# Routed experts of a mixture layer: weight rows dealt to SBUF partitions by neighbours instead of in blocks of 128

## The reference

```python
logits = x @ router_w.T                       # 800 tokens, 8 experts
top_vals, top_idx = jax.lax.top_k(logits, 1)  # one expert for each token
scores = sigmoid(top value for the chosen expert, 0 for the others)
xr = x[None] * scores.T[:, :, None]
gate_up = jnp.einsum('eth,ehf->etf', xr, gate_up_proj)      # 256 -> 2 x 512
gate, up = jnp.split(gate_up, 2, axis=-1)
routed = jnp.einsum('etf,efh->eth', up * silu(gate), down_proj)   # 512 -> 256
shared = silu(x @ shared_gate_w) * (x @ shared_up_w) @ shared_down_w
out = shared + routed.sum(axis=0)
```

## Time and profile before

| what | us |
|---|---|
| median of three runs | 1210.91 |
| the profiled execution, as timed | 1210.05 |
| its span in the profile | 1208.0 |
| PE busy | 1050.0 |
| first gate/up product of tile 0 | at 269.00 |
| first gate/up product of tile 13 | at 355.19 |
| median time from issue to landing, `egu` / `edn` | 5.6 / 6.4 |

### The profile page before, as it was taken

The page is one execution under the profiler, slowest core; times in us unless marked ns, Lnnn a source line. Parts: engine busy times, 40 slices in busy tenths (PEclk is TensorE's granted clock), DMA queues, the critical chain, the costliest instruction groups (busy, mean ns, idle before and its releaser), DMA issues.

```text
span 1208.0 us, 18195 instructions
## 1 busy us (share of the span) xinstructions
PE 1050.0 (87%) x6674; PEld 841.2 (70%) x6674; DVE 530.6 (44%) x1063; ACT 565.0 (47%) x1205; POOL 579.8 (48%) x787
## 2 busy tenths in 40 slices
PE   6986776788882879999999999999999999999883
PEld 3665665457872748888788678778778778877572
DVE  3234552333202663544743653563473473472423
ACT  2322222101212215765765664764665675577761
POOL 2002230244004007767676676676677575376760
PEclk9767887889996969999999999999999999999986
DMA  9015001516761000000000000000000000000000
GB/s 242 4 48 162 1 1 50 197 39 220 269 222 46 1 13 1 1 14 1 1 17 1 1 17 2 1 17 1 1 1 17 1 1 5 1 1 5 1 4 3
DMA packets 37827, 49.25 MB, mean 41 GB/s; under 512 B 9798, under 2 KB 31352, under 8 KB 37484
## 3 DMA queue, kind: packets, MB, share of 16 engines
q1 hardware_dynamic: 36716, 46.46, 12.4%
q0 software_dynamic: 1024, 1.64, 0.4%
HBM read 42.73 MB, written 5.31 MB: 40 GB/s over the span
## 4 chain that ended last, share of the span: by engine, by line
PE 61%; DVE 14%; issue 9%; POOL 6%; ACT 6%; DMA 2%; SPq 0%; POOLq 0%; DVEq 0%; ACTq 0%
PE ps L1033 8%; PE ps L990 5%; PE ps L972 5%; DVE nm L1654 5%; PE ps L913 4%; PE ps L1017 4%; PE ps L1047 4%; PE ps L1044 4%; PE ps L1045 4%; POOL pl L619 3%; PE ps L976 3%; PE ps L1075 2%; PE ps L1066 2%; PE ps L926 2%; PE ps L734 2%
## 5 line engine op out<-in xcount | busy, mean ns | idle before, releaser
L619 POOL TENSOR_TENSOR pl<-pt,ph 120x400 fp32r<-120x400 f32 (+1 forms) x384 | 407.5, 1081 | 282.4 <-ACT ph L1422 238.6
L1421 ACT ACTIVATE pt<-ps 120x400 f32<-120x400 f32 (+1 forms) x384 | 193.8, 505 | 154.3 <-PE ps L1033 150.7
L1654 DVE TENSOR_REDUCE nm<-ps 128x1 f32<-128x482 f32 (+1 forms) x312 | 184.1, 650 | 39.7 <-PE ps L1017 39.1
L1422 ACT ACTIVATE ph<-ps 120x400 fp32r<-120x400 f32 (+1 forms) x384 | 192.0, 500 | 0.0
L1033 PE MATMUL ps<-qh,khl 128*120 128x400 f32 (+1 forms) x384 | 149.7, 390 | 8.8 <-ACT ph L1422 5.6
L1033 PE MATMUL ps<-ql,kh 65*120 65x400 f32 (+1 forms) x384 | 135.1, 352 | 0.0
L1047 PE MATMUL ps<-pl,kv 120*65 120x400 f32 (+1 forms) x384 | 134.2, 349 | 0.4 <-POOL pl L619 0.2
L1044 PE MATMUL ps<-ph,kv 120*65 120x400 f32 (+1 forms) x384 | 134.2, 350 | 0.0
L1045 PE MATMUL ps<-ph,kv 120*64 120x400 f32 (+1 forms) x384 | 133.5, 348 | 0.0
L1017 PE MATMUL ps<-khl,qh 128*128 128x482 f32 (+1 forms) x312 | 101.5, 419 | 6.1 <-DVE ql L1646 1.7
L1633 DVE TENSOR_TENSOR xyz<-ps,ropeq 128x400 f32<-128x400 f32 x64 | 33.8, 570 | 157.3 <-PE ps L976 157.3
(11 more groups left out here) (250 smaller groups left out, 1592.8 us busy)
## 6 DMA issues: line engine op xcount, KB each, us to landing
egu<-_L_ffn_gate_up_proj_dram SPq DMA_DIRECT2D x14, 1024.0 KB, 5.6
edn<-in_L_ffn_down_proj_dram SPq DMA_DIRECT2D x14, 512.0 KB, 6.4
craw<-in_ctx_dram SPq DMA_DIRECT2D x8, 360.0 KB
wo_n<-in_L_xattn_Wo_dram SPq DMA_DIRECT2D x1, 2048.0 KB, 11.7
wq_n<-in_L_xattn_Wq_dram SPq DMA_DIRECT2D x1, 2048.0 KB, 9.7
xs_scratch<-zero SPq DMA_DIRECT2D x1, 1792.0 KB, 12.9
xs<-xs_scratch SPq DMA_DIRECT2D x14, 128.0 KB, 5.5
ys_scratch<-ysb SPq DMA_DIRECT2D x14, 128.0 KB, 5.8
```

Source lines behind the costliest of these rows:

```text
L619: nc.gpsimd.tensor_tensor(pl[k % PS_BUF][r, :], pt[k % PT_BUF][r, :], ph[k % PS_BUF][r, :].bitcast(F32), ALU.subtract).then_inc(pl_ready, 1)
L1421: nc.scalar.activation(pt[k % PT_BUF][0:rows, :], ps[0:rows, k % 2, 0:HT], ACT.Exp)
L1422: nc.scalar.activation(ph[k % PS_BUF][0:rows, :], ps[0:rows, k % 2, 0:HT], ACT.Exp).then_inc(ph_ready, 1)
L1654: nc.vector.tensor_reduce(nm3[0:w, i, n:n + 1], ps[0:w, max_bank(b, i) + n, 0:MN], AX.X, ALU.max)\
```

## The change

Three access patterns of the routed experts change together.

```diff
--- before.py
+++ after.py
@@ -390,8 +390,8 @@
             if t >= EBUF:
                 sp.wait_ge(t_down, t - EBUF + 1)
             e = sp.value_load(owner[0:1, t:t + 1], min_val=0, max_val=NE - 1)
-            sp.dma_start(egu[t % EBUF][:, :, :], gate_up[bass.ds(e, 1)].rearrange("a (c p) n -> p (a c) n", p=128)).then_inc(ld_e[t % EBUF], 16)
-            sp.dma_start(edn[t % EBUF][:, :, :], down[bass.ds(e, 1)].rearrange("a (m p) n -> p (a m) n", p=128)).then_inc(ld_e[t % EBUF], 16)
+            sp.dma_start(egu[t % EBUF][:, :, :], gate_up[bass.ds(e, 1)].rearrange("a (p c) n -> p (a c) n", p=128)).then_inc(ld_e[t % EBUF], 16)
+            sp.dma_start(edn[t % EBUF][:, :, :], down[bass.ds(e, 1)].rearrange("a (p m) n -> p (a m) n", p=128)).then_inc(ld_e[t % EBUF], 16)
 
         def load_slots(sp, t):
 
@@ -896,7 +896,7 @@
                 else:
                     pe.wait_ge(x_shared, B)
                 for c in range(DC):
-                    last = turn(ps[:, 4 + t % 2, TR * c:TR * c + TR], xs[t % XBUF][:, 128 * c:128 * c + 128], ident[:, :])
+                    last = turn(ps[:, 4 + t % 2, TR * c:TR * c + TR], xs[t % XBUF][:, c:D:DC], ident[:, :])
                 last.then_inc(xs_turned, 1)
 
             def expert_in(t, a):
@@ -911,7 +911,7 @@
                 for m in range(FM):
                     for c in range(DC):
                         last = mm(ps[:, 2 * (t % 2) + a, TR * m:TR * m + TR],
-                                  egu[t % EBUF][:, c, FI * a + 128 * m:FI * a + 128 * m + 128], xsT[t % 2][:, c, :],
+                                  egu[t % EBUF][:, c, FI * a + m:FI * a + FI:FM], xsT[t % 2][:, c, :],
                                   start=c == 0, stop=c == DC - 1)
                 last.then_inc(t_up if a else t_gate, 1)
```

## The result

Four runs of the changed kernel took 1247.72, 1244.75, 1248.07 and 1247.99 us, median 1247.86, against a median of 1210.93 for the kernel before (1206.18 to 1216.58, 4 runs). The ratio is 1.0297 with a 95% interval of 1.025 to 1.0344: slower by 37 us. The profiled execution took 1247.72 us. The forecast of 1209.1 and its range of 1200 to 1245 are both missed; rival 1 had 1242.6 (its sum as written, 1210.9 + 45 - 13.4, gives 1242.5).

A forecast was written before the change was run, and what follows sets the result against it. PE bounds the kernel (87% busy), with routed-expert periods set by weight loads. Loads 0.33 us shorter (0.15 + 0.18), half for 11 periods, give 1.8 us: 1210.91 - 1.8 = 1209.1 us against the median, range 1200 to 1245.

The forecast's parts named there:

- rival 1: PE, line 913: stepped load becomes the bound, pairs 220 ns instead of 119, total 1242.6 us; chance 0.26.
- I take 0: Line 913's gate/up operand with 16-byte step: no added cost assumed; bounds nothing to 144 us.
- time for two such reads: PE weight loads: bf16 element every 0.48 ns, fp32 every 0.86, so two reads were said to fit per fp32 element.
- slow clock of tile 3: Line 913 after tile 3's wait: 32 pairs took 5.44 us instead of 3.81; up to 1.63 sparable, taken 0.
- Down weights, 0.15 us a load: Down-weight loads, 1 KB to 4 KB pieces: 1.39 us becomes 1.24, 0.15 off each; bounds 0.12 and 0.25.
- gate/up start, 0.18: Gate/up weight loads, 8 KB pieces: slow start shortened by 0.18 us a load; bounds 0 and 0.77.
- The 1.8 us: Routed experts: total forecast gain, half of 0.33 us a load for 11 periods.
- the half of a load's gain for each period: Routed experts' two-tile loop: half of what a load gets shorter comes off each period, tiles 3 to 13.
- The loop of L and 5.75: Routed experts: period is (L + 5.75) / 2 or 5.59 us, whichever is more; L: down product's end to reloaded tile's start.
- rival 2: Line 913's waits vanish, periods go from 6.70 towards 5.59 us, up to 11.8 + 1.6 off, about 1201; chance 0.14.
- Turns with a step of 8 bytes, 0: Token turns, 28 single loads of 142 ns: no added cost taken; bound 0 to 4 us.
- GpSimd's all-reduce, 0: First all-reduce, starting at 240.80 after 7.92 us of issue: up to 1.6 us gain or as much cost, taken 0.

The follow-up runs named there:

- step of 2: Kernel before the change with only the gate/up operand reading every second column (8 bytes): 1213.05 us, ratio 1.0027.
- step 3: Kernel before the change with only the gate/up operand reading every third column (12 bytes): 1226.51 us, one run.
- experiment 4: Kernel before the change plus 4 KB down-weight pieces and gate/up operand step of 16 bytes; gate/up weights and tokens as before: 1247.19 us, ratio 1.0309.
- experiment 2: Kernel before the change plus larger pieces for both weights and tokens turned with a step; gate/up operand read without step: 1212.14 us, ratio 0.9996.
- experiment 12: Against a kernel issuing gate/up weights a tile earlier (1208.06 us), token loads also issued earlier, ahead of the weights: 1197.97 us, ratio 0.9878.
- experiment 1: Kernel before the change with only the gate/up operand read with a step of 16 bytes: 1246.1 us, ratio 1.030.

## Why the prediction was wrong

**The step that failed is "I take 0" for the gate/up operand with a step of 16 bytes.** It was argued from the bf16 loads' 62 ns for 128 columns, as if the reader could fetch a new address every 0.48 ns. Those columns lie beside each other, 8 to a line of 16 bytes: 16 lines in 62 ns, 3.9 ns for each line. The loads that the prediction set out reach one line in 3.4 ns at best (32 lines in the 110 of the earlier trace rows); the change asks for 128. The row was near by the count of elements, but lines were what had to be counted. Even by elements it fell short of "time for two such reads": 0.86 / 0.48 is 1.8. In place of 0 the step measured 51.0 us of PE time (105.7 - 54.7 for line 913), 236 ns a pair over all 448 (105.7 / 448), 2.0 times the 119 ns pair and 2.1 times the 110 ns load; rival 1 had the factor 2.

The Trainium skill (Advanced Engine Details and Errata, "SBUF Cachelines"), which the prediction set against its own value, was right in kind: different line, penalty. Its sentence that two hits on a line absorb the latency agrees with the step of 2 (126 ns) and with step 3, where two of three lines are hit once only and the price is 63 ns a pair. The runs give it the size that it lacks: 1.8 to 1.9 ns a line.

**Rival 1, point by point.** It had pairs of 220 ns, and 242 were measured in tile 0 (236 over all); 3.2 us more a tile, and 3.90 were measured (7.74 - 3.84); the issue waits of 11.8 us and the slow clock of tile 3 given back, which both happened. With tile 0's time its sum is 14 x 3.90 - 13.4 = 41.2 us, against 38.0 of the stretch; with the busy time of the whole line, in which the slow clock of before is already counted, it is 105.7 - 54.7 - 11.8 = 39.2. It also named the threshold, 30 ns a pair: step 2 (6 ns) stays inside it and costs 0.27%, step 3 (63 ns) is outside and costs 16 us in one run. Its chance of 0.26 was too low, and the range, cut at 1245 against a dearer load, was short by 3.

**Down weights, 0.15 us a load; gate/up start, 0.18.** With loads well apart, by the count over all reloads in experiment 4, 4 KB down weights are worth 0.14 to 0.29 us, and the 8 KB pieces 0.02 more (0.08 by the medians), together 0.16 to 0.31 where 0.33 was forecast. So the term for the down weights is borne out, and the term for the start, a middle between two guesses, is not: hardly anything is left for it. In the kernel's own rhythm (experiment 2) no gain is seen: the same count has a mean of 7.23 us, with two loads of over 9, where it was 6.83 before, and the total is the same to within 4 us. Loads there are issued before the one ahead has landed, as the timeline of experiment 2 shows:

```profile
314.10 0.34 SPq L393 DMA_DIRECT2D egu<-_L_ffn_gate_up_proj_dram  x1
...
314.95 3.81 PE L913 MATMUL ps<-xsT,egu 128*128 128x128 f32 x32 [1.58 <-issue]
...
321.44 0.34 SPq L393 DMA_DIRECT2D egu<-_L_ffn_gate_up_proj_dram  x1
...
321.99 1.24 PE L913 MATMUL ps<-xsT,egu 128*128 128x128 f32 x9 [1.27 <-issue]
```

Tile 7 starts at 314.95, 0.85 us after the weights of tile 8 were asked for, and tile 8 then 7.89 us after the asking. That this overlap eats the gain is likely and was not isolated. The 1.8 us, and with them the half of a load's gain for each period, stay neither shown nor refuted.

**The loop of L and 5.75.** Right as to what the waits are: taking the load out of the loop takes the period to 5.52 (5.59 forecast as PE's own pace) and 13.5 us off the total (11.8 + 1.6 = 13.4 was rival 2's bound). What the prediction did not see is the second wait behind the first: the tokens, asked for after the weights on one queue, which held nearly all of it until experiment 12.

**Turns with a step of 8 bytes, 0.** Right for the time, although the loads themselves got longer (median 209 ns in the changed kernel, 144 in experiment 1): periods with them and without are 9.31 each in the changed kernel and in experiment 1 ((388.35 - 285.90) / 11 and (387.91 - 285.53) / 11). **GpSimd's all-reduce, 0:** it started at 239.70 after 8.35 us of issue in the changed kernel, against 240.80 after 7.92; nothing to tell from noise.

## What to carry to other kernels

Before an operand of PE is given a step, count the 16-byte lines under it, not its elements, and hold lines x 1.8 to 1.9 ns against the time its product has anyway: 64 lines hid under 120 ns, 96 didn't. Longer pieces of a DMA gave 0.2 to 0.3 us a load here and nothing that the total shows, while an earlier issue of the same loads and of the tokens gave 13.5 us; look first at what releases the buffer, and at what is asked for behind the load on the same queue.

## What the runs showed of the hardware that was not expected

The price of a line does not follow PE's clock. Line 913 alone (window; length, busy and count of PE, of PEld; granted clock, DMA share, GB/s), first in the changed kernel, then in the kernel before. The counts take in the products that a window's edges cut:

```profile
269.80:271.80 2.00, 2.00 (x10) 2.00 (x10) 0.50 0.00 0
276.50:278.50 2.00, 2.00 (x10) 2.00 (x10) 1.00 0.00 0
```

```profile
270.00:271.00 1.00, 1.00 (x11) 1.00 (x10) 1.00 0.07 22
288.00:290.00 2.00, 2.00 (x11) 2.00 (x11) 0.50 1.00 408
```

With the step, ten products touch 2 us at a granted clock of 0.50 (1.2 GHz) and ten at 1.00 (2.4 GHz); tile 0, with over 3 us at the lower level, takes 7.74 us and tile 1, wholly at the higher, 7.73. Without it eleven touch 1 us at the higher level and 2 us at the lower, and tile 3, partly at the lower, took 5.44 where others took 3.81. The DMA engines were busy in that last window, but they don't make the difference: tile 13 of experiment 2 took its 5.33 us with the clock at 0.50 and their share at 0.00 (356.10 to 358.40). A price in cycles of PE's clock would have made tile 0 longer than tile 1. So at a step of 16 bytes the pace is set by something that isn't PE's clock, which SBUF's side of the read would be; that it is SBUF's side is a reading, the independence of the clock is what is shown.
